# Mixing stage: the inverse of the denominator from exp(-ln) on ScalarE and one Newton step on VectorE, in place of VectorE's reciprocal

## The reference, cut to what matters

```python
xs = shift(x)                       # the token before
k = einsum(x * tm_k + xs * (1 - tm_k), Wk);  v = ... Wv;  r = sigmoid(... Wr)
def step(carry, kv):                # for every token
    aa, bb, pp = carry
    qt = maximum(pp, kt + u);  e1 = exp(pp - qt);  e2 = exp(kt + u - qt)
    out = (e1 * aa + e2 * vt) / (e1 * bb + e2)       # <- the quotient
    pp_new = maximum(pp + neg_ew, kt)
    f1 = exp(pp - pp_new);  f2 = exp(kt - pp_new)
    return (f1 * aa + f2 * vt, f1 * bb + f2, pp_new), out
ln = layernorm(out) * ln_g + ln_b
s = einsum(r * ln, Wo);  x = x + s * silu(ffn(xn))
```

## Time and profile before

| what | value |
|---|---|
| median of 3 runs | 2034.96 us (2034.64 to 2039.59) |
| the profiled execution: its time, its span | 2031.87 us, 2029.8 us |
| busy over the span: PE, DVE, ACT, POOL | 88%, 64%, 40%, 36% |
| mean granted clock of PE | 0.937 |
| DVE reciprocals of `mix_den` in the mixing stage | 16 of 3327 ns, 53.2 us |
| DVE busy from 690 to 970 us | L1246 is its costliest line there, then the scans L1234 (23.9 us) and L1240 (21.3 us) |

### The profile page before, as it was taken

The page is one execution under the profiler, slowest core; times in us unless marked ns, Lnnn a source line. Parts: engine busy times, 40 slices in busy tenths (PEclk is TensorE's granted clock), DMA queues, the critical chain, the costliest instruction groups (busy, mean ns, idle before and its releaser), DMA issues. The chain is left out here.

```text
span 2029.8 us, 26387 instructions
## 1 busy us (share of the span) xinstructions
PE 1789.8 (88%) x8910; PEld 1427.3 (70%) x8910; DVE 1296.6 (64%) x2000; ACT 802.7 (40%) x1309; POOL 728.3 (36%) x529
## 2 busy tenths in 40 slices
PE   7499999999999788986669978775999999996997
PEld 7388888888888433432337868664899999995885
DVE  4355454444545588999715575662777777775997
ACT  3233333333333346555322211442666666661221
POOL 1244545445454254555312221211222222214554
PEclk9999999999999898988878978778899999997998
DMA  5532323323234401222580122101788888866664
GB/s 190 206 117 100 122 106 112 121 93 124 93 124 150 152 21 51 74 94 93 188 326 27 38 73 110 54 0 60 267 285 295 295 292 293 290 229 217 199 208 143
DMA packets 99364, 306.18 MB, mean 151 GB/s; under 512 B 11920, under 2 KB 13456, under 8 KB 98000
## 3 DMA queue, kind: packets, MB, share of 16 engines
q1 hardware_dynamic: 85280, 259.22, 36.5%
q0 software_dynamic: 14000, 45.89, 7.1%
HBM read 245.82 MB, written 59.24 MB: 150 GB/s over the span
## 5 line engine op out<-in xcount | busy, mean ns | idle before, releaser
L760 DVE TENSOR_TENSOR rows<-rffn_ps_y,rows 128x512 f32<-128x512 f32 x255 | 173.4, 690 | 126.4 <-PE rffn_ps_y L846 123.7
L779 DVE TENSOR_TENSOR rffn_ps_h<-rffn_ps_up,rffn_silu 128x512 f32<-128x512 f32 (+1 forms) x80 | 47.4, 593 | 123.3 <-PE rffn_ps_up L823 123.1
L2021 POOL COPY moe_idx_now<-token_list 128x2 uint32 (+3 forms) x48 | 14.5, 303 | 267.2 <-PE moe_ps_x L2136 267.1
L682 POOL TENSOR_TENSOR rffn_w0l<-rffn_raw,rffn_w0h 128x1536 fp32r<-128x1536 f32 x15 | 52.7, 3514 | 154.3 <-ACT rffn_w0h L703 154.3
L2099 DVE COPY moe_y<-moe_ps_y 128x512 f32<-128x512 f32 x79 | 54.5, 690 | 54.0 <-PE moe_ps_y L2147 50.8
L730 ACT CAST rffn_hT0h<-rffn_ps_h 128x512 fp32r<-128x512 f32 (+1 forms) x48 | 24.8, 516 | 153.2 <-DVE rffn_ps_h L779 123.8
L3107 POOL DMA_INDIRECT att_rows<-ys,pos x64 | 66.9, 1045 | 49.4 <-POOLq L55 32.5
L2026 POOL DMA_INDIRECT moe_x_in<-xn_rows,moe_idx_now x79 | 76.7, 970 | 20.1 <-issue 17.0
L2163 PE MATMUL moe_ps_hidden<-moe_xsh,moe_w_0h 128*128 128x256 f32 (+1 forms) x288 | 80.5, 280 | 3.1 <-DVE moe_w_0l L2103 3.1
L2163 PE MATMUL moe_ps_hidden<-moe_xsh,moe_w_1h 128*128 128x256 f32 (+1 forms) x288 | 80.3, 279 | 1.8 <-issue 1.8
L2163 PE MATMUL moe_ps_hidden<-moe_xsl,moe_w_0h 128*128 128x256 f32 (+1 forms) x288 | 80.7, 280 | 0.0
(11 more groups left out here) (728 smaller groups left out, 6169.6 us busy)
## 6 DMA issues: line engine op xcount, KB each, us to landing
rffn_raw<-in_ffn_w SPq DMA_DIRECT2D x80, 768.0 KB, 4.4
moe_raw<-in_moe_w SPq DMA_DIRECT2D x48, 769.5 KB, 5.8
moe_raw<-in_moe_w SPq DMA_DIRECT2D x48, 768.0 KB, 5.6
ys<-moe_y SPq DMA_DIRECT2D x31, 512.0 KB, 3.2
ahead<-xs SPq DMA_DIRECT2D x17, 256.0 KB, 3.0
ys<-rows SPq DMA_DIRECT2D x17, 256.0 KB, 2.1
ys<-moe_y SPq DMA_DIRECT2D x17, 256.0 KB, 4.1
xT<-front_whole SPq DMA_DIRECT2D x4, 1024.0 KB, 4.4
```

Source lines behind the costliest of these rows:

```text
L682: nc.gpsimd.tensor_tensor(w[b][LO][:], raw[m % 2][:], f32(w[b][HI][:]), ALU.subtract).then_inc(s_w, 1)
L760: nc.vector.tensor_tensor(y[:, t, :], yb[g % 2][:], y[:, t, :], ALU.add).then_inc(s_yadd, 1)
L779: nc.vector.tensor_tensor(hp[:, cols], ub[n % 2][:, cols], sil[n % 2][:, cols], ALU.mult)\
```

## The change

`divide(s)` on DVE no longer takes the reciprocal. ACT makes a rough inverse, exp(-ln(den)), in a new tile `rough` (two buffers) in a new function `guess(s)`: an Ln and an Exp of 128x512. DVE then does one Newton step: t = den*rough, u = (t - 2)*rough (that is minus the better inverse), and wkv = (num * -1)*u. ACT does `guess(s-2)` in step s ahead of `exps(s)`; the last two stand behind the walk.

```diff
+        rough = [a.sb(f"rough{i}", [P, BLK]) for i in range(2)]
+        s_ln = a.sem("den_log")
+        s_ro = a.sem("rough_inverse")
             def divide(s):
                 b, c = s // KC, s % KC
                 dve.wait_ge(s_den, s + 1)
-                nc.vector.reciprocal(den[s % 2][:], den[s % 2][:]).then_inc(s_rc, 1)
-                dve.wait_ge(s_rc, s + 1)
+                dve.wait_ge(s_ro, s + 1)
+                nc.vector.tensor_tensor(den[s % 2][:], den[s % 2][:], rough[s % 2][:], ALU.mult).then_inc(s_rc, 1)
+                dve.wait_ge(s_rc, 2 * s + 1)
+                nc.vector.scalar_tensor_tensor(den[s % 2][:], den[s % 2][:], -2.0, rough[s % 2][:], ALU.add, ALU.mult)\
+                  .then_inc(s_rc, 1)
+                dve.wait_ge(s_rc, 2 * s + 2)
                 dve.wait_ge(s_num, s + 1)
                 if c == 0 and b >= 2:
                     dve.wait_ge(s_o, TPB * (b - 1))
-                nc.vector.tensor_tensor(wkv[b % 2][:, c, :], num[s % 2][:], den[s % 2][:], ALU.mult).then_inc(s_wkv, 1)
+                nc.vector.scalar_tensor_tensor(wkv[b % 2][:, c, :], num[s % 2][:], -1.0, den[s % 2][:], ALU.mult, ALU.mult)\
+                  .then_inc(s_wkv, 1)
...
+            def guess(s):
+                act.wait_ge(s_den, s + 1)
+                need(act, s_wkv, s - 1)
+                nc.scalar.activation(rough[s % 2][:], den[s % 2][:], ACT.Ln).then_inc(s_ln, 1)
+                act.wait_ge(s_ln, s + 1)
+                nc.scalar.activation(rough[s % 2][:], rough[s % 2][:], ACT.Exp, scale=-1.0).then_inc(s_ro, 1)
...
-                if s < STEPS:
-                    exps(s)
+                if s >= 2:
+                    guess(s - 2)
+                exps(s)
...
             walk(step)
+            guess(STEPS - 2)
             high(6)
+            guess(STEPS - 1)
             silu(11)
```

## The result

The changed kernel takes 2038.03 us (median of 20 runs, 2032.07 to 2041.10), the one before 2035.34 (20 runs, 2031.07 to 2039.59) in the same comparison: a ratio of 1.0015 with a 95% interval from 1.0008 to 1.0022, some 3 us slower, and within the 0.3% called no change ahead. The profiled execution has a span of 2033.8 us for 2029.8. The forecast was +4.4 us; from the stage's first MEMSET of `mix_mean_w` to its last `mix_part1l` the profiled executions give 349.88 us for 346.47, +3.4. The other 0.6 of the span lies outside the stage, of it 0.44 ahead of it, where nothing was changed. The 20 runs carry the verdict; a stage is read from one execution, and what such a reading is worth is said with the experiments.

The account below looks back on a forecast made before the run. DVE and PE, both nearly full in the mixing stage, wait for each other at block turns. 2.8 + 0.85 + 1.2 + 0.85 - 0.3 + 0.85 - 1.9 = +4.4 us on 2034.96 gave 2039.3 us, range 2028 to 2045.

Parts of the forecast that it names:

- 1: At `divide(0)`: DVE waits 4.9 us for PE behind it, so a longer quotient costs 0.
- 2: `divide(1..3)`, each 1.0 us longer, push wkv(3), which ended 0.2 us before `mean(0)`: +2.8 us.
- 3: POOL's num comes 0.85 us later, and so do `gate(0)` and the output products DVE waits for: +0.85 us.
- 4: `divide(6)` beside POOL's `diff` ends later, and PE's gates wait for the DVE instruction behind it: +1.2 us.
- 5: `divide(7)` to `divide(9)` stand in front of waits, 0; the second block turn at `gate(1)` costs +0.85 us.
- 6: `divide(10)` gains, -0.3 us; the next two quotients stand before waits again.
- 7: `gate(2)` comes later, +0.85 us; DVE's scan waits for it, so `divide(13)` is hidden.
- 8: Last two quotients, POOL's work mostly past: wkv(15) ends at T + 7.25 for 9.15, moving `mean(3)` and the tail: -1.9 us.
- B: Rival: POOL keeps its place when its next instruction is ready, biting at `divide(2)` and `divide(6)`: +8.3 us, 2043.3 us; chance 0.20.
- C: Rival: DVE gets its three turns in a row, quotients 1.0 us shorter, num 1.8 later: about -1.5 us, 2033.5; chance 0.20.
- D: Rival: nothing excludes anything, the change does what its durations say: about -7 us, 2028; chance 0.12.
- E: Rival: ACT becomes late and moves `squares` and `gate`: some +6 to +12 us; chance 0.03.

Follow-up runs that it names:

- dve_only: Changed kernel's three DVE instructions with `rough` a constant 1.0 and no guess on ACT: 2037.54 us, ratio 1.0010 to the kernel before.
- act_only: Changed kernel with ACT's guess kept and waited for, but DVE taking the reciprocal as before: 2035.87 us, ratio 0.9991 to the kernel before.
- pool_waits: Changed kernel with POOL's `quotient(s)` waiting until `divide(s-1)` is done: 2058.7 us, ratio 1.0115 to the kernel before.
- newton_1: Kernel before with the new quotient form in `divide(1)` alone: 2037.06 us, ratio 1.0001 to the kernel before.
- tail_newton: Kernel before with the new quotient form for the last two quotients only, reciprocal for the first 14: 2032.51 us, ratio 0.9986 to the kernel before.
- early_newton: Changed kernel with `divide(s-2)` moved ahead of `sums(s-1)` for c = 0, 1 and 2: 2039.32 us, ratio 1.0019 to the kernel before.
- early_no_newton: Changed kernel without the Newton step and with `divide(s-2)` ahead of `sums(s-1)` for c = 0, 1, 2: 2030.20 us, ratio 0.9976 to the kernel before.
- no_newton: Changed kernel without the Newton step, wkv = num * rough as one product: 2030.95 us, ratio 0.9977 to the kernel before.
- newton_23: Kernel before with the new quotient form in `divide(2)` and `divide(3)` alone: 2035.35 us, ratio 0.9995 to the kernel before.
- early_recip: Kernel before, reciprocal kept, with `divide(s-2)` moved ahead of `sums(s-1)` for c = 0, 1 and 2: 2045.67 us, ratio 1.0053 to the kernel before.

## Why the prediction was right, and where not

The main step held: the three new instructions take turns with POOL's four, a quotient right behind `sums` is longer and not 1.8 us shorter, and the places where DVE is waited for are few. Shown by the timeline of step 5, by dve_only (cost without ACT), by act_only (no cost without DVE's part), and by pool_waits (the instructions fall to 0.66 to 0.69 when POOL is not beside them). The size of the term was a little off. In the eight steps where the quotient stands right behind `sums` its end moved from T + 4.00 to T + 4.79, or from 4.18 to 4.97: 0.79 us, for a forecast of 1.0 that set its T + 5.1 against 4.0. The same 0.79 is found in step 8, and where other work of DVE lies between the scan and the quotient it is 0.1 to 0.3 us shorter, but 0.1 longer in `divide(14)`. The rule of the Trainium skill (SBUF — State Buffer, the section on what contends) that was weighed there agrees in that the two exclude each other; the order in which they take turns is from the rows.

The shifts, changed minus before, each against its own stage's start and read at the start or end of the instruction named:

| step of the prediction | forecast | measured | read at (before, after) |
|---|---|---|---|
| 1, 2: to `mean(0)` | +2.8 | +2.0 | 762.16, 764.59 |
| 3: to `gate(0)` | +0.85 | +0.8 | 798.07, 801.30 |
| 4: `divide(6)` ends | +1.2 | +0.8 | 821.13, 825.13 |
| 5: to `gate(1)` | +0.85 | +0.8 | 876.30, 881.08 |
| (none): `output(1)` ends | 0 | +1.0 | 893.14, 898.96 |
| 6: to `mean(2)` | -0.3 | -0.3 | 915.49, 921.00 |
| 7: to `gate(2)` | +0.85 | +0.8 | 948.60, 954.89 |
| 8: wkv(15) ends | -1.9 | -1.85 | 966.40, 970.84 |
| (none): to the stage's end | 0 | -0.6 | 1019.56, 1023.41 |
| sum | +4.4 | +3.4 | |

**The step that was wrong is 2**, in its mechanism, and by more than the 0.8 of the table. I wrote that `divide(1)` to (3) push the end of wkv(3) and that `mean(0)` starts 0.2 us behind it. But the four parts of `mean(0)` wait each for their own wkv, and the one that needs wkv(3) is last; so wkv(3) had some 2.6 us more. What moves `mean(0)` is `divide(1)`: behind it on DVE stands `peak(4)`, for which PE waits before the next key products (`key(6)`), and from there PE runs without a stop to `mean(0)`. That wait grew by 0.79 (4.39 for 3.60 us below), just as much as `divide(1)` itself, which is also what newton_1 shows. The other 1.2 us are a longer `key(6)`, and nothing shows that the change brings it. First before, PE's timeline at `key(6)`:

```profile
739.87 5.27 PE L1527 MATMUL mix_ps_k<-mix_mix,mix_w 128*128 128x512 f32 x8 [3.60 <-DVE mix_e L1223]
```

and the window there, columns as in the earlier trace rows:

```profile
738.00:752.00 14.00, 12.13 (x25) 5.37 (x26) 13.79 (x15) 4.76 (x6) 8.06 (x5) 0.88 0.26 75
```

then the changed kernel, timeline:

```profile
741.04 6.55 PE L1545 MATMUL mix_ps_k<-mix_mix,mix_w 128*128 128x512 f32 x8 [4.39 <-DVE mix_e L1226]
```

and window:

```profile
738.00:752.00 14.00, 10.96 (x19) 4.80 (x20) 13.79 (x15) 8.59 (x10) 7.14 (x6) 0.76 0.26 75
```

The same eight products take 6.55 us for 5.27, and the clock granted over the window is 0.76 for 0.88, a mix of its two levels (1.2 and 2.4 GHz) with more of the lower one (0.76 as well over 739.2 to 753.2, which starts as far from `key(6)` as the window before). But tail_newton, which up to there does the work of the kernel before and waits as long, has the longer `key(6)` too:

```profile
743.43 6.45 PE L1553 MATMUL mix_ps_k<-mix_mix,mix_w 128*128 128x512 f32 x8 [3.60 <-DVE mix_e L1226]
```

The forecast had no term for this. With the right chain of waits and nothing for the clock, step 2 would have been +0.8 and the whole forecast +2.4. That the sum came within a microsecond is in part luck: a wrong chain of waits put 2.0 us too much into step 2, and PE's products put 1.2 back there and 1.0 at `output(1)`, of which the forecast knew nothing. Of the +3.4 that were measured, about 1.85 come from the steps with their right waits.

**Step 4** was mis-sized, 0.8 for 1.2: the quotient ended at T + 6.83 (825.13 - 818.30), not T + 7.2. `diff` held DVE's third instruction for 1.75 us (from 822.83, the end of the second, to 824.58), not its whole 1.9, and the turns ahead of it were a little shorter than written. **Not in the forecast** are the +1.0 at `output(1)`, where PE's 32 products began 4.8 us later and ended 5.8 later, with a granted clock of 0.91 for 1.00 over the 20 us around them, and the -0.6 behind the last quotient, of which 0.35 are sixteen products of `output(3)` that took 9.02 us for 9.37. Neither has an experiment of its own, and what brings them stays open.

**The rivals.** B (POOL keeps its place) falls: `divide(2)`, for which it had T + 8.8, ended at T + 4.98 (752.29 - 747.31), and in step 8 DVE got in between the two `diff` instructions. C (three turns in a row) and D (no exclusion) fall with the same timelines. E falls with act_only. ACT's guess in step 7, timeline of the changed kernel:

```profile
786.10 1.28 ACT L1444 ACT_TABLE_LOAD   x1
787.39 0.63 ACT L1444 ACTIVATE mix_rough<-mix_den 128x512 f32<-128x512 f32 x1
788.04 1.28 ACT L1446 ACT_TABLE_LOAD   x1
789.33 0.63 ACT L1446 ACTIVATE mix_rough<-mix_rough 128x512 f32<-128x512 f32 x1
789.87 0.70 ACT L1436 ACTIVATE mix_e<-mix_e,mix_ew 128x512 f32<-128x512 f32 x1
```

That is 3.8 us (789.87 - 786.10; forecast 4.0), taken out of the wait for `peak`, 36.7 us in the earlier trace rows and now:

```profile
ACT mix_e L1436 <- DVE mix_e L1226: 13.4, 5, 3.5
```

The Trainium skill (ScalarE: Activation LUTs, What ACT_TABLE_LOAD costs) names a drain on top of each load, by which the guess would be an estimated 6.7 us. The 1.29 us from a load's start to the next instruction show none here, and the measurement decides.

The absolute figure, 2039.3, also took the median of three runs as its base. The 20 runs put before at 2035.34 and the changed kernel at 2038.03: the base was 0.4 us too low, the change 1.7 too high by the medians and 1.0 too high by the stages of the profiled executions.

## What to carry to other kernels

Before a long instruction with one SBUF input is replaced by several short ones with two, look at what the other engine of the shared memory does beside it: under the reciprocal's 3.3 us POOL worked freely, and the new form pays where POOL is idle (the last two quotients end 1.86 us earlier against the scan, and the kernel with it there alone has a ratio of 0.9986). When a step is moved out of the other's way, list who waits for what now comes later; here `peak` waited for POOL's num, 52.4 us in pool_waits and 16.5 in early_newton, and neither was faster than the kernel before. And for "who is pushed by this", read which instruction waits for which part: a group of products that begins 0.2 us behind a result needn't need that result first.

## What the runs showed of the hardware

DVE and POOL take turns instruction by instruction when both have two-input work in SBUF: the ends alternate at 0.55 and 1.1 us, even where POOL's next instruction is ready (step 8). The `blend` of the earlier trace rows waited for two `gate` instructions in a row instead; what makes that difference wasn't tried. A reciprocal, with one input, is not part of this: 3.32 to 3.34 us in all 16, with POOL's quotient beside it or not.

PE's restart behind a wait has no fixed length, even for the same code and the same wait: the stage's first eight products took 5.16 to 6.67 us. The eight products of `key(6)` take, in the twelve profiles: after a wait of 2.12 us 3.70 (early_no_newton) and 5.40 (no_newton); after 3.60 us 5.27 (before), 5.26 (act_only) and 5.12 (newton_23), but 6.42 (early_recip) and 6.45 (tail_newton); after 4.37 us and more never under 6 (6.47 dve_only, 6.55 changed, 6.75 newton_1, 6.08 early_newton, 6.36 pool_waits). After 2.12 and after 3.60 us more than one length is seen for the same wait. Whether a longer wait makes the longer time likelier, as five of five against two of five may suggest, isn't shown; what decides it stays open. A difference of 1.2 us at one such place is a third of this change's effect, which is why waits and durations, and not the times, part the theories above.
